# Moving one low-half subtraction behind two key products in the attention steps of VectorE

## The reference

```python
x = x + attn_a(layernorm(x))        # row 1 of x @ W + b, broadcast over the sequence
x = x + ffn(layernorm(x))           # sigmoid(xr @ W_r) * (square(relu(xk @ W_k)) @ W_v)
x = x + attn_b(layernorm(x))
x = x + ffn(layernorm(x))

# attn_b: 16 heads of 64 columns, blocks of 128 rows
q, k = rope(x @ Wq.T + bq), rope(x @ Wk.T + bk);  v = x @ Wv.T + bv
scores = q_block @ [k_previous_block, k_own_block].T / 8      # 128 x 256, banded mask
ctx = softmax(scores) @ [v_previous_block, v_own_block]
out = merged_heads(ctx) @ Wo.T + bo
```

## Time and profile before

| | |
|---|---|
| profiled execution | 1637.48 us, the same as the median of the three runs |
| its span (first to last instruction) | 1635.7 us, so 1.8 us lie around it |
| VectorE (DVE) busy | 1482.5 us, 91% of the span |
| TensorE (PE) matmuls busy | 1489.2 us, 91% |
| ScalarE (ACT) busy | 1261.5 us, 77% |
| GpSimd (POOL) busy | 968.6 us, 59% |
| L1268, low halves of the probabilities, 256 times | 339.3 us, mean 1326 ns |
| L1061, transposes of the probabilities, 256 times | median 4.8 us from issue to landing |

### The profile page before, as it was taken

One profiled execution on the slowest core, in us unless ns is written; L12 is line 12 of the kernel. 1 busy time (PEld: TensorE's weight loads), 2 busy tenths in 40 slices (PEclk: granted clock), 3 DMA queues, 4 the chain that ended last, 5 costly groups with the idle time before them and its releaser, 6 DMA issues. The chain is left out here.

```text
span 1635.7 us, 46118 instructions
## 1 busy us (share of the span) xinstructions
PE 1489.2 (91%) x16674; PEld 1129.9 (69%) x16674; DVE 1482.5 (91%) x4009; ACT 1261.5 (77%) x2266; POOL 968.6 (59%) x786
## 2 busy tenths in 40 slices
PE   5999977899999999999989999999999999869998
PEld 4888745666666766666766666676666666658887
DVE  5999689899999999999999999999998999957885
ACT  5999667777778787778777777877777777749996
POOL 4665357665666666666667566666665666513443
PEclk7999999899999999999999999999999999979999
DMA  5233247989899989999998989999989899971331
GB/s 209 91 123 107 78 90 132 172 147 188 152 184 166 178 154 177 172 170 176 171 174 155 182 154 184 166 185 162 174 162 157 159 165 160 163 164 63 113 107 75
DMA packets 721528, 247.86 MB, mean 152 GB/s; under 512 B 687380, under 2 KB 706072, under 8 KB 721304
## 3 DMA queue, kind: packets, MB, share of 16 engines
q1 hardware_dynamic: 720600, 244.53, 77.2%
q10 hardware_dynamic: 704, 0.40, 0.1%
HBM read 47.73 MB, written 25.17 MB: 45 GB/s over the span
## 5 line engine op out<-in xcount | busy, mean ns | idle before, releaser
L1457 ACT ACTIVATE at_prob<-at_prob,at_top 128x256 f32<-128x256 f32 (+1 forms) x1024 | 429.0, 490 | 110.8 <-DVE at_top L1256 107.5
L1256 DVE CUSTOM_DVE_ANT_0 at_prob<-banks,at_masks,pre_s_scale 128x256 f32<-128x256 f32 (+1 forms) x1024 | 420.2, 470 | 18.3 <-PE banks L1685 4.1
L1268 DVE TENSOR_TENSOR at_halves<-at_prob,at_halves 128x1024 f16<-128x1024 f32 (+1 forms) x256 | 339.3, 1326 | 0.7 <-ACT at_halves L1466 0.7
L1685 PE MATMUL banks<-at_kt,at_qt 32*128 32x256 f32 (+1 forms) x4096 | 256.4, 387 | 57.5 <-DVE at_top L1256 20.3
L1580 PE MATMUL banks<-at_xt,pre_w_h 128*128 128x512 f16 x1024 | 297.0, 383 | 5.1 <-DVE at_v_l L1330 4.3
L1685 PEld LDWEIGHTS banks<-at_kt,at_qt 32*128 32x128 f32 x4096 | 205.7, 189 | 117.5 <-issue 116.2
L1202 POOL TENSOR_TENSOR at_c_halves<-at_ctx,at_c_halves 128x1024 f16<-128x1024 f32 x64 | 136.6, 2135 | 253.4 <-DVE at_halves L1268 233.7
L1466 ACT ACTIVATE at_halves<-at_prob 128x1024 f16<-128x1024 f32 (+1 forms) x256 | 263.6, 1030 | 7.7
L1638 PEld LDWEIGHTS banks<-at_v_h,at_pt 128*128 128x128 f16 x1984 | 181.8, 98 | 86.3 <-issue 61.7
L1638 PE MATMUL banks<-at_v_h,at_pt 128*128 128x65 f16 x1984 | 208.6, 195 | 34.0 <-DVE at_ctx L1283 21.8
L1171 POOL TENSOR_TENSOR at_kt<-at_k_by 128x512 f32<-128x512 f32 x128 | 163.1, 1274 | 90.6 <-DVE at_halves L1268 90.5
(11 more groups left out here) (124 smaller groups left out, 3222.9 us busy)
## 6 DMA issues: line engine op xcount, KB each, us to landing
f_x<-in_x SPq DMA_DIRECT2D x16, 512.0 KB, 3.9
x_after_ffn<-f_x SPq DMA_DIRECT2D x16, 512.0 KB, 2.6
at_x_ln<-x_after_ffn SPq DMA_DIRECT2D x16, 512.0 KB, 4.5
at_x_res<-x_after_ffn SPq DMA_DIRECT2D x64, 128.0 KB, 2.8
x_after_attention<-at_x_res SPq DMA_DIRECT2D x64, 128.0 KB, 2.8
f_x<-x_after_attention SPq DMA_DIRECT2D x16, 512.0 KB, 4.6
out_x<-f_x SPq DMA_DIRECT2D x16, 512.0 KB, 3.0
at_tables<-in_cos SPq DMA_DIRECT2D x16, 256.0 KB, 3.8
```

The lines of the kernel that those rows point to most:

```text
L1256: last = nc.vector.tensor_tensor_reduce(out=prob[:, n % 2, h, low:2 * P], in0=s_ps[:, h, n % 2 * 2 * P + low:(n % 2 + 1) * 2 * P], in1=mas ...
L1268: nc.vector.tensor_tensor(parts[:, 1, :, :], prob[:, n % 2, :, keys_from(t, b):2 * P], parts[:, 0, :, :], ALU.subtract).then_inc(p_low, 1)
L1457: last = nc.scalar.activation(at, at, ACT.Exp, bias=top[:, n % 2, h:h + 1], scale=-1.0)
L1685: last = nc.tensor.matmul(s_ps[:, h, d * 2 * P + keys_from(t, b):(d + 1) * 2 * P] .rearrange("p (s t) -> p s t", t=P), qt[rows_of, par, ha ...
```

## The change

In `at_step` of `vector`, the call `p_low_of(t, 2)` moves from ahead of `key_product(t + 2, 1)` and `key_product(t + 2, 2)` to behind them. No operation is added, removed or resized, no other engine's order changes, and `last_step` is untouched.

```diff
             v_low_of(t + 1, 0)
             context(t, 0)
-            p_low_of(t, 2)
             key_product(t + 2, 1)
             key_product(t + 2, 2)
+            p_low_of(t, 2)
             if g == 3 and S > -2:
                 x_low_of(S + 2)
             p_low_of(t, 3)
```

## The result

Four timed runs of the changed kernel gave 1657.19 to 1660.17 us, median 1658.49. The kernel before gave a median of 1637.93 us beside them. The ratio is 1.0122, with a 95% interval of 1.0104 to 1.0142: the change costs 20 us, where 4 were forecast and 1651 was the upper end of the range. The profiled execution was the quickest of all, 1650.62 us with a span of 1648.8, 13 us over that of before, so its rows show less than the usual loss.

A forecast was written before the change was run, and what follows sets the result against it. VectorE's work and a once-a-quad transpose chain through SyncE were taken as the bounds. Nine quads at +0.5, four at -0.36 and +1.1 at the start summed to +4.2 us: 1641.7 us, range 1629 to 1651.

The forecast's parts named there:

- the third step's wait: Product pair's wait for TensorE in the third step, claimed gone: its place begins at 1034.25, behind TensorE's 1034.10.
- The stall beside GpSimd: VectorE's L1268, up to 2066 ns beside GpSimd's L1181; claimed to fall to about 1.2 to 1.3 us.
- The delay of block 2 in the first step: Block 2's low half ends 1.14 us later in a first step, delaying its transpose and those queued behind in SyncE.
- The second and third step: VectorE over both steps together: -0.03 us in a quad with the output wait; 0.49 us saved in one without.
- a quad with the wait: Quad whose second step waits for TensorE's output, nine of 13; round changes by +0.34 to +0.55 us, 0.5 taken.
- the start: Start of the attention stage, where the pair already waited 0.64 us: the low half now comes after it, +1.1 us.
- The fourth step: VectorE from the moved place to what follows: 2.53 us against 3.30, so -0.77 us.
- the full queue: SyncE's queue full back to the fourth step, so the round starts there: +0.55 us a quad instead of +0.34.
- Absorbed: Rival: SyncE's queue swallows block 2's delay, giving -10.1 us, 1627.4 us; chance 0.27.
- Every step pays: Rival: later transposes delay values products and the pair in the other steps too, +11.7 us more, 1653.4 us; chance 0.12.
- the four quads without the wait: Quads where the output was ready 0.24 us early: a 1.09 us wait opens against 1.45 saved, -0.36 us each.
- The rule weighed against the rows: Estimate from 261 GB/s: the chain's four transposes take 8 us and swallow the delay; the trace's 13.4 us was preferred.

The follow-up runs named there:

- first_only: The change made only in the first step of each quad, against the kernel before: 1652.51 us, ratio 1.0087.
- queue_waits: VectorE's order of before; SyncE alone waits for the second key product ahead of block 2's transpose in every step: 1657.13 us, ratio 1.0113 to the kernel before.
- x_late_after: The change together with the transpose of x issued one step later in each quad, against the kernel before: 1632.59 us, ratio 0.9961.
- light_after: The change, with only the high halves of the contexts transposed from the third group of blocks on, against the kernel before: 1626.41 us, ratio 0.9921.
- middle_only: The change made only in the second and third step of each quad, against the kernel before: 1644.93 us, ratio 1.0029.
- light_middle: The change in the second and third step only, with the shorter context transposes, against the kernel before: 1629.30 us, ratio 0.9940.
- fourth_only: The change made only in the fourth step of each quad, against the kernel before: 1634.04 us, ratio 0.9980.
- middle_queue_waits: VectorE's order of before; SyncE delays block 2's transpose in the second and third step only: 1638.53 us, ratio 1.0001 to the kernel before.

## Why the prediction was wrong, point by point

The direction was right, and so was the mechanism of the first step; the size was five times too small. The step that failed is the working for the second and third step, which had the third step's wait gone; beside it the fourth step's saving was sized too large. By the prediction's own terms:

- **The stall beside GpSimd.** Right. L1268's longest row fell to 1353 ns, its mean over all 256 from 1326 to 1212 ns, and VectorE's busy time in the stage by 21 us.
- **The delay of block 2 in the first step, 1.14 us into the round.** Right in size too. The same working for the first step alone gives 9 x 1.14 + 4 x (1.09 - 0.19) = +13.9 us; first_only measured 1652.51 - 1638.6 = +13.9. queue_waits, x_late_after and light_after confirm the path. So close an agreement is partly luck, since the interval is about 2.5 us wide to either side.
- **The second and third step, -0.03 a quad with the wait, -0.49 without, +1.1 at the start: -1.1 us in all.** This term failed: middle_only measured +6.3 (4.8 by the ratio). The working said that in the third step the pair's wait "is gone", because VectorE comes later to its place while TensorE ends `keys_of` at 1034.10 as before. TensorE does not stay put. `tops` stand behind the pair and both low halves, so the pair's new wait in the second step makes them later, and TensorE's `scores` wait for `tops`. In the profile after that wait is 0.50 us at 1114.08, 7.59 us after the second step's place (1106.49). Before, the same scores started 7.06 us after the place (1015.78) without a wait:

```profile
1022.84 1.53 PE L1685 MATMUL banks<-at_kt,at_qt 32*128 32x256 f32 x21
```

  The last group of L1580 follows: 18.25 us after the place (1124.74), for 17.72 before (1033.50). TensorE is thus later by the 0.53 us that pass between the place and the pair (1107.02 - 1106.49), and the pair still waits for it in the third step, 0.29 us here and 0.15 to 0.29 us in all 14 quads. The two steps take 21.39 us in place of 20.95. In a quad without the wait of `residual` they took 1113.64 - 1092.24 = 21.40 before already, so nothing is lost or gained there. The two rows of before, from VectorE's timeline:

```profile
1092.24 1.66 DVE L1268 TENSOR_TENSOR at_halves<-at_prob,at_halves 128x1024 f16<-128x1024 f32 x1
...
1113.64 1.21 DVE L1268 TENSOR_TENSOR at_halves<-at_prob,at_halves 128x1024 f16<-128x1024 f32 x1
```

  That makes 9 x 0.44 + 1.1 = +5.1 us. In light_middle, where `residual` waits only 2.0 us in 4 waits, little more than the start's 1.1 should be left. 1.3 was measured, which fits but is within the intervals. The start's 1.1 us was not measured by itself.
- **The fourth step, -0.77 a quad: -10.0 us.** Mis-sized: fourth_only measured -4.6 (-3.3 by the ratio). The saving in its place is 0.66 us a quad, 8.6 us; the rest is given back behind it. In fourth_only TensorE waits for `at_pt` three times as long as before (16.6 us for 5.3). In the profile after, the quad shown has such a wait, 0.99 us at 1084.30, and behind it VectorE waits 0.44 and 0.71 us at the end of the first step. That quad is one of the dearer ones: the pair's wait there is 0.71 us in 3 of 14 quads and 0.15 to 0.29 us in the others. That the queue is full from the fourth step on I had only as a difference of 0.16 us a quad. With lighter transposes the step gives 6 to 8 us, so the full queue is a part of the loss; the runs leave open whether it is all.
- **The sum.** The parts alone measured 13.9 + 6.3 - 4.6 = 15.6 us, and the whole 20.6. Of the 16.4 us between forecast and result, 7.4 lie in the second and third step, 4.0 in the fourth (forecast -10.0 and +1.4 for the full queue), and 5.0 in no part alone. These 5 us are either that the parts hinder one another in the full queue or the spread of four intervals; no run tells which.
- **The rivals.** *Absorbed* falls: queue_waits and first_only show the delay passed on in full. *Every step pays* is nearest in time, 1653.4 us, but not in its mechanism: I had the later transposes cost the other steps 0.3 us each, and middle_queue_waits shows that in the second and third step they cost nothing. The at_pt waits it named did come (22.9 us for 5.3), and the prediction had named them as a sign against itself; first_only (12.8 us) and fourth_only (16.6) have more of them than middle_only (9.2). Its chance, 0.12, was too low, and the range ended 7 us below the measured time. In the sum of *Absorbed* the four quads without the wait should have had the 0.77 + 0.19 + 0.49 = 1.45 us of the main working and not 1.0, which makes it 1.8 us faster and changes nothing in the verdict.
- **The rule weighed against the rows.** By the prediction's estimate from the 261 GB/s of the Trainium skill (DMA: Bandwidth & Descriptors, section Latency and other measured facts) the four transposes take 8 us and leave room for the delay. The traces do not agree: in the quads of both kernels they take 11.9 to 14.9 us until the output starts. And the runs decide for the rows: 1.3 us more in front of block 2's transpose in every step cost 18.5 us over the stage.

## What to carry to other kernels

An operation that feeds a transfer is not placed by what it costs its own engine: follow the queue from it to the next wait of the busiest engine before moving it, since here 21 us less of busy time were paid for with 34 us of waiting. Where two bounds meet once in a round, what shortens the round pays for both orders (a transpose moved out of it gave 8 us here, and cut the change's cost from 20 us to 3.5, which the intervals do not tell from nothing), and gains measured one by one need not add up. And when a work estimate says "this wait is gone because the other engine stays where it was", check what that other engine waits for next: here it came 0.53 us later, by just what the first engine had lost.

## What the runs showed of the hardware

VectorE's subtraction with both inputs in SBUF stands nearly as long as GpSimd's operation beside it lasts (0.84 us longer for 0.98 us together, 0.45 for 0.58), while a product with one input in PSUM did not lengthen. After the change the pair at 1144.52 keeps its pitch of 1.32 us, though GpSimd runs beside it until 1145.32; its row there, from the timeline of the changed kernel:

```profile
1142.82 2.50 POOL L1181 TENSOR_TENSOR at_qt<-at_q_by 128x512 f32<-128x512 f32 x2
```

The four transposes of the round took 12.6 to 14.9 us before and 11.9 to 13.9 us after, from the first issue to the start of the output, and the changed kernel's executions spread by nearly 10 us (1650.62 to 1660.17), which one profiled execution does not show.
